# Row maxima of the first attention head: three of five products copied to half precision by ScalarE and folded pairwise by VectorE

## The reference

```python
attn = jnp.einsum('bqc,bkc->bqk', q * scale, k)          # 12 heads, 2304 queries, 2304 keys, head width 16
attn = (attn.reshape(B * nh, H, W, H, W) + rel_h[:, :, :, :, None] + rel_w[:, :, :, None, :]).reshape(B * nh, H * W, H * W)
attn = jax.nn.softmax(attn, axis=-1)
out = jnp.einsum('bqk,bkc->bqc', attn, v)
```

## Time and profile before

| | us |
|---|---|
| median of 3 runs | 1040.89 |
| lowest and highest | 1038.16, 1045.59 |
| the profiled execution | 1040.68 |
| its span, first to last instruction | 1038.8 |
| PE, DVE, ACT, POOL busy | 999.6, 848.4, 701.1, 338.5 |
| list `before` on TensorE, first product to first scores | 98.50 to 123.54 |

### The profile page before, as it was taken

The page is one execution under the profiler, slowest core; times in us unless marked ns, Lnnn a source line. Parts: engine busy times, 40 slices in busy tenths (PEclk is TensorE's granted clock), DMA queues, the critical chain, the costliest instruction groups (busy, mean ns, idle before and its releaser), DMA issues.

```text
span 1038.8 us, 36808 instructions
## 1 busy us (share of the span) xinstructions
PE 999.6 (96%) x15944; PEld 704.1 (68%) x15944; DVE 848.4 (82%) x1746; ACT 701.1 (67%) x1005; POOL 338.5 (33%) x162
## 2 busy tenths in 40 slices
PE   7888999999999999999999999999999899899998
PEld 5565267777776777777676777777647777675666
DVE  5769999999999999999999999999925767243664
ACT  4776177778787777778777777877775455241665
POOL 5530142322435352433425242322314456100211
PEclk9985599999999999999999999999999999999999
DMA  5787754443413231313132221311200011222231
GB/s 142 209 202 235 218 139 134 130 110 73 107 53 98 59 97 50 99 43 99 48 86 65 71 79 52 91 55 56 62 26 13 24 31 30 82 60 77 81 92 58
DMA packets 75168, 91.80 MB, mean 88 GB/s; under 512 B 15351, under 2 KB 67388, under 8 KB 74815
## 3 DMA queue, kind: packets, MB, share of 16 engines
q1 hardware_dynamic: 74977, 89.45, 31.6%
q10 hardware_dynamic: 30, 0.02, 0.0%
HBM read 65.63 MB, written 23.21 MB: 86 GB/s over the span
## 4 chain that ended last, share of the span: by engine, by line
PE 79%; DVE 9%; DMA 4%; ACT 4%; issue 2%; POOL 2%; SPq 0%; DVEq 0%; ACTq 0%
PE ps L1202 41%; PE ps L1373 20%; PE ps L1197 13%; DVE mx_p L1692 2%; DVE stage_lo L1661 1%; ACT hid_f L1124 1%; PE ps L1215 1%; DVE stats L94 1%; DMA rel<-in_c_rel_h 1%; POOL rstd L120 1%; PE ps L1319 1%; DVE xh L112 1%; PE ps L1544 1%; PE ps L1567 1%; DMA xin<-in_x 1%
## 5 line engine op out<-in xcount | busy, mean ns | idle before, releaser
L1692 DVE TENSOR_REDUCE mx_p<-ps 128x1 f32<-128x464 f32 (+1 forms) x1080 | 606.7, 627 | 15.9 <-PE ps L1202 5.8
L1071 ACT ACTIVATE prob<-ps 128x768 f32<-128x768 f32 x648 | 495.3, 810 | 165.8 <-PE ps L1202 165.4
L1202 PE MATMUL ps<-kc,qc 112*32 112x464 f16 (+1 forms) x4320 | 455.9, 369 | 3.0 <-DVE stage_lo L1661 2.9
L1202 PE MATMUL ps<-qv,ka 113*32 113x384 f16 x5184 | 400.2, 327 | 2.6 <-ACT prob L1071 2.3
L852 POOL COPY qv<-qv 48x6144 f16<-48x6144 f16 x36 | 190.8, 5300 | 352.7 <-DMA qv<-kq_d 352.3
L1373 PE MATMUL ps<-prob,v_ext 128*32 128x384 f32 x2592 | 289.8, 487 | 0.0
L1202 PEld LDWEIGHTS ps<-qv,ka 113*32 113x32 f16 x5184 | 213.0, 97 | 77.9 <-issue 19.6
L1202 PEld LDWEIGHTS ps<-kc,qc 112*32 112x32 f16 x4320 | 171.2, 95 | 101.1 <-DVE mx_p L1692 27.7
L1373 PEld LDWEIGHTS ps<-prob,v_ext 128*32 128x32 f32 x2592 | 116.6, 111 | 12.4 <-ACT prob L1071 1.0
L1197 PE MATMUL ps<-xnt_all,w_up 96*128 96x384 f16 x432 | 75.0, 326 | 2.8 <-ACT hid_f L1124 2.8
L120 POOL TENSOR_TENSOR rstd<-rstd 96x4 f32<-96x4 f32 x23 | 26.5, 1152 | 139.6 <-DVE rstd L102 139.1
(11 more groups left out here) (117 smaller groups left out, 818.0 us busy)
## 6 DMA issues: line engine op xcount, KB each, us to landing
qv<-rel_d SPq DMA_DIRECT2D x216, 144.0 KB
qc<-rel_d SPq DMA_DIRECT2D x22, 216.0 KB, 4.0
xin<-in_x SPq DMA_DIRECT2D x12, 288.0 KB, 4.1
kq_d<-khl SPq DMA_DIRECT2D x24, 144.0 KB, 2.6
q_h<-kq_d SPq DMA_DIRECT2D x9, 288.0 KB, 4.6
q_w<-qw_d SPq DMA_DIRECT2D x9, 288.0 KB, 6.4
rel_d<-stage_hi SPq DMA_DIRECT2D x4, 648.0 KB, 9.0
rel_d<-stage_lo SPq DMA_DIRECT2D x4, 648.0 KB, 10.8
```

Of the source, the lines that this page charges most:

```text
L1071: nc.scalar.activation(prob[:, s4(p, s), :].rearrange("p (a b) -> p a b", a=2), ps[:, 3 + 2 * (s % 2):5 + 2 * (s % 2), 0:CW], ACT.Exp).the ...
L1202: ins = nc.tensor.matmul(ps[c:c + 32, bank, 0:w], l[:, c:c + 32], r, start=True, stop=True, tile_position=(0, c))
L1692: nc.vector.tensor_reduce(mx_p[:, q * GT + k // MP, k % MP:k % MP + 1], ps[:, slot, 0:min(MW, N - k % MP * MW)], AX, ALU.max).then_inc(uni ...
```

## The change

Of the five products of a query tile, two (the fourth and the fifth, k = 3 and 4) stay max units in the ring of three banks. The other three go to banks 3 to 6 in turn. ScalarE copies each of them into a half precision buffer in SBUF, `mcopy` (three query tiles deep, three parts of 464 columns each). VectorE takes the elementwise maximum of the first two parts, then of that and the third (called folds here), and reduces the 464 columns to one column of `mx_p`. Columns 1 and 2 of `mx_p` are set once, near the kernel's start, to -3.0e38. This holds for the nine query tiles of the list `before` alone. ScalarE issues its two transfers between copies.

```diff
@@ -144,6 +144,8 @@
 
         with ExitStack() as r:
             khl = sb("khl", [C2, 2, 4, 2, CW], F16, r)
+        with ExitStack() as r:
+            mcopy = sb("mcopy", [128, 3, 3, MW], F16, r)
         with ExitStack() as r:
             x3t = sb("x3t", [128, 2, 3, C], F32, r)
             y_o = sb("y_o", [128, 3, C], F32, r)
@@ -440,8 +447,26 @@
             return [u for x in range(2 * STEPS) for u in units_of(n)[x]]
 
 
-        before = [("max", 0, k) for k in range(GU)] + [("max", 1, k) for k in range(LEAD)]
-        before.insert(GU + 1, ("mt", 0, 0))
+        before, copied, steps, reds = [], [], [], []
+        for i in range(GT + LEAD // MP):
+            group, t = i // GT, i % GT
+            folds = [("fold", (i, 0)), ("fold", (i, 1)), ("fold", (i, 2))]
+            for k in (0, 1, 3, 2, 4) if i else (3, 0, 1, 2, 4):
+                if k < 3:
+                    steps.append(("copy", len(copied)))
+                    copied.append((group, t * MP + k))
+                    continue
+                last = (group, t, k) == (0, GT - 1, MP - 1)
+                if last:
+                    reds += folds
+                for unit in [("max", group, t * MP + k)] + [("mt", 0, 0)] * ((group, t, k) == (1, 0, 3)):
+                    steps.append(("unit", len(before)))
+                    reds.append(("unit", len(before)))
+                    before.append(unit)
+                if not last:
+                    reds += folds[:1] if k == 3 else folds
+                    folds = folds[1:]
+        TILES = len(copied) // 3
         U_HEAD = len(flat(1))
         U_ALL = len(before) + len(flat(0)) + (NH - 2) * U_HEAD + len(flat(NH - 1)) + 1
         PAIRS = STEPS // 2
@@ -1038,11 +1063,28 @@
                 act.wait_ge(op_ps, tile + 1)
                 out_hi, x = operand_tiles(s, i)
                 nc.scalar.activation(out_hi[0], x, ACT.Copy).then_inc(op_hi, 1)
+            for c in range(2):
+                act.wait_ge(k_out[c], 32 * NC // 2)
+                act.wait_ge(q_rows_out[c], 32 * NC // 2)
+            act.wait_ge(qw_ok, 2 * NC)
+
+            def copy_scores(i):
+
+                act.wait_ge(copy_ps, i + 1)
+                wait_used(act, pair_red, i // 3 - 2)
+                nc.scalar.activation(mcopy[:, i // 3 % 3, i % 3, :], ps[:, 3 + i % 4, 0:MW], ACT.Copy).then_inc(copy_ok, 1)
+
+            for i in range(3 * GT):
+                copy_scores(i)
             act.wait_ge(unit_ok, before.index(("mt", 0, 0)) + 1)
             act.dma_start(m_d[0].rearrange("(k t) -> k t", t=128), mneg[:, :]).then_inc(m_out, 16)
+            for i in range(3 * GT, 3 * GT + 2):
+                copy_scores(i)
             act.wait_ge(m_out, 16)
             act.dma_start(qv[QR:QR + 1, 0, :, :],
                           m_d[0:1, :].unsqueeze(1).to_broadcast([1, NV, QW])).then_inc(qv_in[0], 16)
+            for i in range(3 * GT + 2, 3 * TILES):
+                copy_scores(i)
             act.wait_ge(q_first, 32)
             act.wait_ge(q_rest, 32)
 
@@ -1341,8 +1383,21 @@
                 pe.wait_ge(norm["out"], c + 1)
                 transposes(xh2[0], bank).then_inc(done, 1)
 
-            for u, unit in enumerate(before):
-                ring_unit(0, 0, unit, u, u % RING)
+            def copied_scores(i):
+
+                group, k = copied[i]
+                wait_used(pe, copy_ok, i - 3)
+                qt, w = group * GT + k // MP, k % MP * MW
+                mm_quarters(3 + i % 4, MW, qc[0][0:HD + 2 * S, qt * 128:(qt + 1) * 128],
+                            kc[0][0:HD + 2 * S, w:w + MW]).then_inc(copy_ps, 1)
+
+            pe.wait_ge(c_in[0], 64)
+            for kind, i in steps:
+                if kind == "copy":
+                    copied_scores(i)
+                else:
+                    ring_unit(0, 0, before[i], i, i % RING)
+            pe.wait_ge(copy_ok, 3 * TILES)
             pe.wait_ge(v_one, 1)
             pe.wait_ge(onehot_k_in[0], 80)
             pe.wait_ge(sel_in, 16)
@@ -1631,6 +1686,7 @@
 
             norm1(0)
             norm1(1)
+            nc.vector.memset(mx_p[:, 0:2 * GT, :], -3.0e38).then_inc(mx_neutral, 1)
 
             def table_parts(i):
                 dve.wait_ge(rel_h16, i + 1)
@@ -1682,9 +1738,22 @@
                            lambda: wait_used(dve, t2_ps, c), beside_root)
 
 
+            def folded(i, part):
+
+                x = mcopy[:, i % 3, :, :]
+                if part < 2:
+                    dve.wait_ge(copy_ok, 3 * i + part + 2)
+                    wait_used(dve, pair_max, 2 * i + part)
+                    nc.vector.tensor_tensor(x[:, 0, :], x[:, 0, :], x[:, part + 1, :], ALU.max).then_inc(pair_max, 1)
+                else:
+                    dve.wait_ge(pair_max, 2 * i + 2)
+                    nc.vector.tensor_reduce(mx_p[:, i, 0:1], x[:, 0, :], AX, ALU.max).then_inc(pair_red, 1)
+
             def ring_unit(n, p, unit, count, slot):
                 kind, group, k = unit
                 q = group % NQ
+                if is_at(n, 0) and group < 2 and kind == "max" and k == GU - 1:
+                    dve.wait_ge(pair_red, TILES if group else GT)
                 dve.wait_ge(unit_ps, count + 1)
                 if kind == "max":
                     if k == 0:
@@ -1718,8 +1787,12 @@
                         projected(0, 0)
                     ring_unit(n, p, unit, units_before(n) + u, ring_slot(n, p, u))
 
-            for u, unit in enumerate(before):
-                ring_unit(0, 0, unit, u, u % RING)
+            dve.wait_ge(mx_neutral, 1)
+            for kind, i in reds:
+                if kind == "fold":
+                    folded(*i)
+                else:
+                    ring_unit(0, 0, before[i], i, i % RING)
             period(0, 0)
             period(1, 1)
             for i in range(1, NH // 2 - 1):
```

More of the change, by code:

```diff
@@ L301, in build @@
         mx_red = sem("mx_red")
+        mx_neutral = sem("mx_neutral")
+        copy_ps = sem("copy_ps")
+        copy_ok = sem("copy_ok")
+        pair_max = sem("pair_max")
+        pair_red = sem("pair_red")
         m_out = sem("m_out")
```

## The result

The changed kernel takes 1044.72 us (median of 20 runs, 1040.82 to 1049.78), the kernel before beside it 1040.86 (20 runs). The ratio is 1.0037, 95% interval 1.0025 to 1.0049: 3.9 us slower, and less than the 1% that the prediction took as its bound. The forecast was 1045.0 us. The profiled execution took 1045.49 us with a span of 1043.7, 4.9 more than the span of the earlier trace rows.

A forecast was written before the change was run, and what follows sets the result against it. VectorE was taken to bound the list `before`, TensorE the periods. Terms -3.1 + 0.87 + 4.6 + 0.4 + 0.1 + 2.0 = 4.9, less 0.6, gave +4.3 on 1040.68: 1045.0 us, range 1039.5 to 1047.5.

The forecast's parts named there:

- (b): Rival for the folds' price: one column a cycle, 0.65 us instead of 0.40, 18 times, +4.5, giving 1049.5; chance 0.08.
- (c): Rival for the SBUF reduction: two columns a cycle, 0.41 us, -2.0 over nine tiles, giving 1043.0; chance 0.05.
- first tile's wait: First query tile of the list: its first fold waits for two ScalarE copies, +0.87 us.
- hold: Second tile: its first fold is held until GpSimd's copy of qv ends at 107.64, +4.6 us.
- (a): Rival: folds and GpSimd's qv copy pass each other, so 4.6 and 0.4 fall away, giving 1040.0; chance 0.2.
- (d): Rival: VectorE and GpSimd both go at half speed during the copy, +1.6 instead of 4.6, giving 1041.6; chance 0.05.
- v_ext: Fifth tile: its first fold falls on two GpSimd copies from 114.78 to 115.57, +0.4 us (bounds 0 and 0.8).
- sixth tile: Sixth tile of the list: its two folds stand on end, which means one more wait, +0.1 us.
- gap behind it: Behind mneg: the next fold starts 1.6 us late, with ScalarE's copies behind its transfer; mt unit +2.0 in all.
- hidden: Row of qv before the scores: landed by +3.7, ahead of the last copy at +5.4, so no cost.
- last term: Start of the period: scores 2.7 late, VectorE's list 4.9 late, its old 0.7 us of idleness used up: -0.6.
- Rival (e): TensorE's clock might rise to 2.4 GHz before the scores, changing only the -0.6, by at most 0.4; inside the forecast.

The follow-up runs named there:

- e1: Changed kernel with the second and third query tile reduced from PSUM in five units instead of folded; 1.0003 of the kernel before.
- e3: Changed kernel with GpSimd making its first copy of qv twice, one behind the other; one run, 1047.59 us to 1039.99 for the kernel before.
- e5: Changed kernel with GpSimd's first copy of qv cut into eight instructions of 768 columns, each waiting for the one before; 1.0016 of the kernel before.
- e9: e7 with 16 matmuls that nobody reads ahead of the wait for the last copy; 0.9988 of the kernel before.
- e11: e10 without the held SyncE stores and with 14 unread matmuls instead of 8; 1039.39 us, 0.9978 of the kernel before.
- e7: Changed kernel with the edits of e1 and e4 together; 1.0003 of the kernel before.
- e2: Changed kernel without folds: one reduction over all 1392 copied columns of a tile; one run, 1042.56 us to 1039.99 for the kernel before.
- e10: Changed kernel with e5's pieces, e4's copy order, SyncE's late stores held until the row of qv landed, 8 unread matmuls; 1.0033 of the kernel before.
- e4: Changed kernel with ScalarE making copies 18 and 19 before its wait for mneg, 20 and 21 between its transfers; 1.0028 of the kernel before.
- e8: Changed kernel with the first three tiles reduced from PSUM, e4's order, SyncE's late stores held until the row of qv landed; 1.0024 of the kernel before.

## Why the prediction was right, and where it wasn't

**Steps that held.** A fold took 0.39 us (forecast 0.40), the SBUF reduction 0.64 (0.63), a tile 2.37 (2.38), so rivals (b) and (c) are out. The first tile's wait cost 0.86 (0.87). The hold cost 4.57 (4.6), and e1, e3 and e5 show that it was the copy's; it caught the second fold of the second tile instead of the first, since the copy began 0.21 later and the list 0.62 earlier, which changes nothing in the sum. Rivals (a) and (d) are out. `v_ext` cost 0.24 (0.4), the sixth tile 0.33 (0.1). `mneg` ended 22.28 us behind the list's start (the forecast's 120.8 - 98.5 is 22.3). The gap behind it was 1.71 (1.6).

**Steps that failed, two that may belong together.** The prediction put the row of `qv` as "hidden". TensorE was through with its products at 124.96, and the last copy ended where forecast; the row came at 126.3, 4.1 us after its issue ended. The 1.4 us of the first transfer was taken for the second. For SyncE's stores the prediction found room in the DMA share of 0.34 from 123.50 to 127.40, which is the wrong stretch: where the row travels, the trace of before has 0.99.

```profile
119.50:123.00 3.50, 3.50 (x28) 0.67 (x24) 3.50 (x7) 0.00 (x0) 0.00 (x0) 0.50 0.99 290
```

Itself this cost 0.8 us at the start of the scores. The Trainium skill (DMA: Bandwidth & Descriptors, "Latency and other measured facts") gives an HBM access latency of 0.2 us on average and 2 us at high load. The row goes the same way, slower at high load, and by more: 4.1 us from the end of its issue with the stores, 1.7 without.

The larger part is the last term, forecast at **-0.6**: VectorE's old idleness would be used up. VectorE ended its list 4.4 us late against the list's start (forecast 4.9), so this sum was near; 0.3 of the rest is idleness that the kernel before already had behind `mneg` (14 units in 7.9 us, where 14 x 0.545 is 7.6). But from there to the second `mx` it took 10.99 us instead of 9.40 (124.83 to 134.23 before): **+1.6**. The clock had fallen to 0.50 for 6.2 us of that stretch, behind TensorE's wait of 1.38 us for the row; in the kernel before it was at half for 2.5. e9 and e11, with the wait filled, take 8.4. Rival (e) had the clock as able to rise early, "at most 0.4"; that it can then fall again, and what waits would do to it, was not in any case. The term is off by 2.2 us, where the forecast's own range left 1.0 upwards. That the late row made the clock fall is the likely link between the two steps, as e7 and e9 show it for a wait of 2.84 us; for the 1.38 us of the changed kernel no run isolates it, and the size is that of one profiled execution.

**Why the number is near all the same.** The second `mx` is 6.0 us late against the list's start, where the terms said 4.3. The list began 0.6 earlier in this profile, and 0.5 came back behind the second `mx` and in the rest of the span: 4.9. The median rose by 3.9. The terms were short by 1.7 us, and the other differences happened to go the other way. As the start of the list differs by up to 5.4 us between profiles, this closeness is in part luck; what the chip confirmed is the hold and the tile's price, not 1045.0 to the tenth.

**Where the expected saving went.** A folded tile takes 2.37 us instead of 2.73, so the nine do save about 3.1. In the changed kernel the costs are the first tile's wait (0.9), the hold (4.6), `v_ext` and the sixth tile (0.6), the gaps at the mt unit (1.9) and the stretch of half clock (1.6): 9.6 - 3.1 is 6.5, less the 0.3 of idleness that was there before, and the measured lateness of the second `mx` is 6.0. Even e11, without the hold, the gap and the half clock, keeps only 1.0 of the 3.1 at the end of VectorE's list.

## What to carry to other kernels

Before VectorE gets an instruction with two SBUF sources, look up in the timeline what GpSimd runs in that stretch and how long its *single* instructions are: the hold is one whole instruction, so cutting it in pieces with a wait between them, or a reduction of one source in place of the folds, gives nearly all of the hold back. When a stretch gets faster, list what the next one still waits for (a small transfer beside large stores, the clock after TensorE's wait), since the gain stops there. And a store that is held back for a critical transfer holds back everything behind it on its queue, which may be needed 20 us later.

## What the runs showed of the hardware

- The held fold ended 0.26 us behind GpSimd's copy in the changed kernel (108.19 and 107.93).
- A half precision elementwise maximum of 464 columns out of SBUF takes 0.39 us, a reduction of 464 columns 0.64 and of 1392 columns 1.59 (e2). From the two reductions a column costs 0.95 / 928 = 1.02 ns, an estimate; by it 464 columns are 0.48 of the 0.64.
- The granted clock stood at 0.99 from 104 to 107 us although TensorE was busy for 0.80 of 3.00 us there, and it was 0.50 from 108 to 124. In e10 an idle time of 0.95 us at full clock left it at 1.00. Behind the 1.38 us of the changed kernel and the 2.44 of e4 it fell to 0.50 when the scores were already running again; in the 2.84 us of e7 it fell during the wait. What exactly decides between these was not tried.
- Beside two stores of 648 KB a transfer of 13.5 KB landed 4.1 us behind the end of its issue (changed kernel, e7), and 1.7 us with the stores held back (e8, e10).
